# Two attention products beside transposes of heads, and W_v's mean beside block 0's plain gram

## What is computed

```python
# feed-forward (twice, with the same weights, added with 0.5)
xr = mu_r * x + (1.0 - mu_r) * x_prev          # x_prev: the token before
xk = mu_k * x + (1.0 - mu_k) * x_prev
out = sigmoid(xr @ W_r.T) * (square(relu(xk @ W_k.T)) @ W_v.T)
# attention, 16 heads of 16, added with 1
q, k = relu(proj(Wq)) / scale, relu(proj(Wk)) / scale
v, u = proj(Wv), silu(proj(Wu))
kv  = einsum('bhlk,bhlv->bhkv', k, v)          # over the whole batch
out = einsum('bhlk,bhkv->bhlv', q, kv)         # the attention product
out = srms_norm(out) * u                        # norm by head
return out @ Wo.T
```

## Time and profile before

| | us |
|---|---|
| median of 3 runs | 306.01 |
| lowest and highest | 305.83, 307.62 |
| the profiled execution | 305.97 |
| its span (first to last instruction) | 304.20 |
| PE busy, share of the span | 297.3, 98% |
| DVE / ACT / POOL busy | 245.9 / 236.0 / 210.8 |
| TensorE's granted clock | full in all 40 slices |
| chain that ended last: PE / DVE / ACT | 85% / 8% / 3% |

### The profile page before, as it was taken

How to read it: one execution, slowest core, us unless ns; L and a number is a source line. 1 busy time by engine, 2 the same in 40 slices (tenths; PEclk the granted TensorE clock), 3 DMA queues, 4 the chain that set the end, 5 groups by cost and what they waited for, 6 DMA issues and landing times.

```text
span 304.2 us, 5777 instructions
## 1 busy us (share of the span) xinstructions
PE 297.3 (98%) x2003; PEld 272.1 (89%) x2003; DVE 245.9 (81%) x601; ACT 236.0 (78%) x462; POOL 210.8 (69%) x236
## 2 busy tenths in 40 slices
PE   6999999999999999999999999999999999999995
PEld 5888889988998999999988998999999999999894
DVE  4899996776976876985992998687989888999695
ACT  3988959969779589598178267489797979699981
POOL 4498969789489478577277117636797979759923
PEclk9999999999999999999999999999999999999999
DMA  7950040130210400000000000000010101002123
GB/s 243 377 209 3 1 140 0 32 108 0 72 70 0 137 3 2 0 1 2 0 3 0 2 0 0 2 2 2 0 40 33 54 19 66 5 0 72 46 95 138
DMA packets 16128, 15.05 MB, mean 49 GB/s; under 512 B 738, under 2 KB 15076, under 8 KB 16100
## 3 DMA queue, kind: packets, MB, share of 16 engines
q1 hardware_dynamic: 15808, 14.42, 14.3%
q10 hardware_dynamic: 292, 0.26, 0.3%
HBM read 8.39 MB, written 6.29 MB: 48 GB/s over the span
## 4 chain that ended last, share of the span: by engine, by line
PE 85%; DVE 8%; ACT 3%; issue 1%; DMA 1%; POOL 1%; DVEq 0%; ACTq 0%
PE psK L1344 8%; PE psK L1346 8%; PE psK L1345 8%; PE psX L1344 8%; PE psX L1346 8%; PE psX L1345 8%; PE psRV L1344 8%; PE psRV L1346 7%; PE psRV L1345 7%; PE psA L1361 3%; PE psA L1549 2%; PE psX L1562 2%; PE psX L1476 2%; PE psK L1549 2%; DVE mix L994 2%
## 5 line engine op out<-in xcount | busy, mean ns | idle before, releaser
L994 DVE SCALAR_TENSOR_TENSOR mix<-psA,mu,mix 128x512 f32<-128x512 f32 x60 | 41.5, 744 | 10.7 <-ACT mix L676 10.7
L459 POOL TENSOR_TENSOR mix_k_lo<-mix,mix_k_hi 128x512 fp32r<-128x512 f32 x26 | 33.6, 1313 | 5.1 <-ACT mix_k_hi L709 5.0
L676 ACT ACTIVATE mix<-psA,one_mu 128x511 f32<-128x511 f32 x60 | 36.9, 698 | 0.0
L1344 PE MATMUL psRV<-ffn_hi,mix_r_hi 128*128 128x256 f32 x120 | 34.3, 286 | 0.0
L1346 PE MATMUL psRV<-ffn_hi,mix_r_lo 128*128 128x256 f32 x120 | 33.6, 280 | 0.0
L1345 PE MATMUL psRV<-ffn_lo,mix_r_hi 128*128 128x256 f32 x120 | 33.5, 279 | 0.0
L659 ACT ACTIVATE xn<-xs,shiftA,rstdA 128x256 f32<-128x256 f32 x53 | 27.9, 627 | 1.9 <-POOL shiftA L443 1.9
L1344 PE MATMUL psRV<-ffn_hi,act_hi 128*128 128x256 f32 x96 | 27.4, 286 | 0.0
L1346 PE MATMUL psRV<-ffn_hi,act_lo 128*128 128x256 f32 x96 | 26.8, 279 | 0.0
L1345 PE MATMUL psRV<-ffn_lo,act_hi 128*128 128x256 f32 x96 | 26.8, 279 | 0.0
L963 DVE BATCH_NORM_STATS2 statsA<-xs 128x6 f32<-128x256 f32 x64 | 22.4, 411 | 2.6 <-DMA xs<-x_dram 2.5
(11 more groups left out here) (212 smaller groups left out, 1093.5 us busy)
## 6 DMA issues: line engine op xcount, KB each, us to landing
xs<-x_dram SPq DMA_DIRECT2D x7, 512.0 KB, 7.9
out_dram<-xs SPq DMA_DIRECT2D x7, 512.0 KB, 2.8
spread<-xn SPq DMA_DIRECT2D x8, 256.0 KB, 3.4
squares<-spread SPq DMA_DIRECT2D x8, 256.0 KB, 2.7
out_dram<-xs SPq DMA_DIRECT2D x4, 128.0 KB, 1.7
xs<-x_dram SPq DMA_DIRECT2D x2, 128.0 KB, 2.7
xs<-x_dram ACTq DMA_DIRECT2D x2, 128.0 KB, 3.0
silu_u<-w_ffn_k_dram SPq DMA_DIRECT2D x1, 256.0 KB, 4.0
```

The source lines that it names most:

```text
L459: nc.gpsimd.tensor_tensor(mix_k_lo[:, h, :], mix[:, 0, h, :], mix_k_hi[:, h, :].bitcast(F32), ALU.subtract).then_inc(s_lo_k, 1)
L676: nc.scalar.activation(mix[:, rk, h, 1:BLOCK], psA[:, h, 0:BLOCK - 1], ACT.Copy, scale=one_mu[:, rk, h:h + 1]).then_inc(s_prev, 1)
L994: nc.vector.scalar_tensor_tensor(out=m, in0=psA[:, h, :], scalar=mu[:, rk, h:h + 1], in1=m, op0=ALU.mult, op1=ALU.add).then_inc(s_mix, 1)
L1344: nc.tensor.matmul(dst, a_hi, b_hi, start=start, stop=False)
```

## The change

- `attend(1)` is called right behind `transpose_g(0)`, in front of `ffn_v(6)`, where it stood behind `gram(5)`.
- `attend(2)` is called right behind `transpose_g(1)`, in front of `ffn_v(7)`, where it stood behind `project_out(1)`.
- W_v's mean is made in stage 1, behind `gram(0)`: GpSimd's sum two calls earlier in the same loop step, VectorE's subtraction at the end of step 1 and not 3, and the waits that go with it.

```diff
@@ gpsimd @@
                 if i == 2:
                     pool.wait_ge(s_wo_hi, 1)
                     nc.gpsimd.tensor_tensor(wo_lo[:], wo[:], wo_hi[:].bitcast(F32), ALU.subtract).then_inc(s_wo_lo, 1)
+                if i == 1:
+                    weight_sum("v")
                 scales_b(i)
                 x1_low(i)
-                if i == 1:
-                    weight_sum("v")
@@ vector @@
-                    turn(i + 1, {4: [(s_wcen, 4)], 5: [(s_kvbd, 1)]}.get(i, ()))
+                    turn(i + 1, {5: [(s_kvbd, 1)]}.get(i, ()))
...
                 r_low(i + 1)
-                if i == 3:
+                if i == 1:
                     center_weight("v", 4)
@@ tensor @@
                 if name == "v":
 
-                    pe.wait_ge(s_halo, 6)
+                    pe.wait_ge(s_halo, 4)
...
             gram(0)
+            weight_mean("v")
             q_of(0, (s_silu, 2))
...
                 ffn_v(i)
-                if i == 3:
-                    weight_mean("v")
                 gram(i - 1)
...
             transpose_g(0, [(s_silu, 22)])
+            attend(1, [(s_halo, 9)])
             ffn_v(6)
             project_out(0)
             gram(5)
-            attend(1, [(s_halo, 9)])
             q_of(5, (s_x2, 2))
...
             transpose_g(1, [(s_silu, 26)])
+            attend(2, [(s_gu, 4)])
             ffn_v(7)
             project_out(1)
-            attend(2, [(s_gu, 4)])
             q_of(6, (s_x2, 4))
```

## The result

The changed kernel took 310.75 us in the median of six runs (308.74 to 312.54), the kernel before 305.92 us beside it (305.51 to 307.65). The ratio of the times on record is 1.0113, 95% interval 1.0074 to 1.0151: slower by a little over 1%. (It is not the quotient of the two medians, which is 1.0158. I had put down 309.2 us; the profiled execution is there to 0.02 us, but the median of all six is 1.6 us above it and outside my range.

What follows compares the result with a forecast made beforehand. TensorE's own list was taken to bound the kernel; 0 (W_v's mean) + 1.42 (attend(1)) + 1.78 (attend(2)) = 3.20 us over the profiled 305.97 gave 309.17, with a range for 8 in 10 of 307.6 to 310.0.

Steps and rivals of the forecast that it cites:

- What bounds the kernel: Whole kernel: TensorE, busy in 98% of the span, bounds it; edits count only through group cost or TensorE's waits.
- No gain from plain products side by side: At both moved attend calls: a plain-fp32 group beside another saves nothing, bounds 0 and 0.1 us each.
- W_v's mean at 0: Behind gram(0): GpSimd's sum falls into its 2.35 us wait for statistics; cost 0, bounds 0 to 0.2 us.
- attend(1), +1.42 us: Stage 6: keep_g(5) and VectorE's chain to x2_low(6) run later; TensorE's k_and_u(6) load waits, +1.42 us, bounds 1.1 to 1.8.
- attend(2), +1.78 us: Stage 7: the whole shift reaches TensorE, about 1 us each at transpose_a(8) and k_and_u(7); +1.78 us, bounds 1.4 to 1.9.
- Rival 1, the collision at r_low(7): Stage 6: GpSimd's x1_low(6) gets between VectorE's two r_low(7) operations, chain 0.60 us longer; 309.8 us, chance 0.08.
- Rivals 2, 3: 2: only the stage 7 wait comes, 307.8, chance 0.13; 3: not slower, VectorE catches up before both loads, 305.7, chance 0.05.
- Rival 4, the clock behind the waits: At TensorE's three new waits: the clock falls to 1.2 GHz behind one or two, 310.7 to 312.2 us; chance 0.05.

Runs made afterwards that it cites:

- reordered kernel: The changed kernel with VectorE's gate_heads(1), gate_heads(2) and the first half of head_sums(2) called earlier; median 307.43 us of 12 runs, ratio 1.0006 to the kernel before.

## Why the prediction came out as it did

- **What bounds the kernel**: right. Only what made TensorE wait counted; the 12 us that ScalarE no longer waits for `attend` came to nothing.
- **No gain from plain products side by side**: right. The change's TensorE busy time is 297.8 us, not less than before. `attend(1)`, now beside transposes, takes 143.14 - 141.43 = 1.71 us to the first matmul behind it, where the kernel before has 1.70. The reordered kernel, which has all of the early products and none of the waits, is no faster.

```profile
141.43 1.95 PE L1549 MATMUL psA<-kv_bd,q_store 128*128 128x128 f32 x16
143.14 0.36 PE L1344 MATMUL psRV<-ffn_hi,act_hi 128*128 128x256 f32 x1
```

- **W_v's mean at 0**: right. The sum did meet VectorE's add, as I had allowed for: it took 1.17 us and not 0.74. TensorE didn't wait for it all the same: the last of the loads of `gram(0)` starts at 38.03 + 2.56 - 0.19 = 40.40, and the mean's load 0.22 us behind it, the step that the loads of `gram(0)` have among themselves (timelines of PEld, DVE and POOL of after).

```profile
38.03 2.56 PEld L1510 LDWEIGHTS psK<-k_tok,xs 128*128 128x128 f32 x12
...
38.81 1.04 DVE L1077 TENSOR_TENSOR xs<-xs,gate 128x512 f32<-128x512 f32 x1
...
39.26 1.17 POOL L500 TENSOR_TENSOR wsum<-wv 128x256 f32<-128x256 f32 x1
...
40.62 0.41 PEld L1583 LDWEIGHTS psA<-wsum,mean_w 128*128 128x128 f32 x2
```

- **attend(1), +1.42 us**: 1.41 us in the trace, 0.07 of them from before the wait, 1.27 and 1.57 us by time. `keep_g(5)` was forecast at 151.84 and came at 151.90, the end of `x2_low(6)` at 162.00 and 161.99.
- **attend(2), +1.78 us**: 3.20 - 1.41 = 1.79 us in the trace, 1.69 and 1.72 us by time. Both waits, about 1 us each, came where they were put.
- **Rival 1, the collision at r_low(7)**: it didn't come. VectorE's pair took its 1.29 us, and GpSimd was the one that stood back, 2.98 us for `x1_low(6)` where it took 2.5 elsewhere:

```profile
153.20 2.98 POOL L507 TENSOR_TENSOR x_lo<-xs,x_hi 128x512 fp32r<-128x512 f32 x2
```

The rule that the prediction took from the Trainium skill's "GPSIMD Engine Reference" (the table under Specifications), contention over SBUF interfaces shared with VectorE, agrees with this and with the 1.17 us of the sum. That entry doesn't settle who stands back. In both rows it was GpSimd, which had started inside VectorE's instruction; in the earlier trace rows it was VectorE, which had started inside GpSimd's.
- **Rivals 2, 3**: refuted by the loads at 162.11 and 185.18. **Rival 4, the clock behind the waits**: the granted clock is 1.00 from 140 to 192 us, well inside what the record of the clock covers, and the load of `k_and_u(7)` comes 3.20 us late, with no remainder for slower work.
- **What failed**: the step from the profiled execution to the median. I took them as 0.04 us apart because the median of three runs of before lay so, and gave the top of the range, 310.0, to a rival in stage 6. The third of those runs, 307.62, was in the table: a second kind of run, 1.7 us longer, which about half of all later runs of before belong to. The prediction also took the clock as full in every slice of the earlier trace rows, where the record of it begins at 7.17 us: the first term of the span that differs from run to run had no place in the sum. With the second kind of run the range would have reached to 310.9 and the chance of over 1% would have been higher than 0.53. The sum itself was right for the runs in which the clock rises early. That the profiled execution of the changed kernel was one of these, as that of before was, is luck; 8 of its 12 runs were not.

## What to carry to other kernels

An earlier producer is worth something only if a reader's own list is changed with it; here the readers of the three products that were pushed back sat ahead of the early product's reader on VectorE. When a group moves ahead of others on the engine that bounds, follow each of the others to its reader, and from there down that engine's list to the next thing that the bounding engine waits for: the air at that one place (in stage 6 0.36 us: VectorE's wait of 0.16, and 0.20 between the end of `x2_low(6)` and the load beyond the 0.12 that it needs; in stage 7 none) is what the move has to fit into. And look at the spread of the runs before putting a range on a median.

## What was not expected of the hardware

The moment at which TensorE's clock rises differs between runs of one kernel: 5.34 us in one trace of the changed kernel and 10.24 in another, 11.66 at the latest over all traces. It showed as 16 matmuls in 5.31 and not 3.69 us, in about half of the runs. A page that prints full clock from the first slice doesn't show it; the spacing of the matmuls does. Six transposes of fill in front of the first products took the late starts from 18 of 35 runs to none of 12, and to 1 of 12 in another kernel, by a way that is open. The three waits of 0.9 to 1.3 us in the middle of the changed kernel had no such effect: the record has the clock full from 5.34 to 305.72 us.
